# A state-space stage whose convolution moves into TensorE's projection, with the products dt·u·B split between VectorE and GpSimd

## Chip, cores and metric

The kernel runs on one core of a Trainium2 chip. The metric is device time in microseconds (us) of one execution. VectorE (DVE), ScalarE (ACT), GpSimd (POOL) and TensorE (PE) each run their own instructions in order and wait for one another by semaphores.

## What is computed

The program is a decoder of two layers over x of 32 sequences x 128 tokens x 128 channels: attention with 16 heads of 8 channels, a linear-attention block, routed experts, then a state-space layer, attention over a context, and a second set of experts. The change touches the first attention and the state-space layer:

```
# first attention, per head h of 8 channels: rotate q and k, then
scores = q_h @ k_h.T + causal mask ;  softmax ;  @ v_h

# state space, 256 inner channels d, 16 states n, 4 taps
x_in, z = split(layernorm(x) @ W_in)
xc = silu(depthwise_conv(x_in, 4 taps) + conv_b)
dt, B, C = from xc @ W_xproj ;  dt = softplus(dt @ W_dt + b_dt)
h[d,n] = h[d,n] * exp(dt[d] * A[d,n]) + dt[d] * B[n] * xc[d]     # over tokens
y[d] = sum_n h[d,n] * C[n]
out = x + ((y + xc * D) * silu(z)) @ W_out
```

## The kernel before

All six stages keep x in SBUF and take it in 8 groups of 4 sequences (512 tokens). A stage ends with a barrier of all engines.

**State space** (`state_space`, from L1165). The 256 channels are two halves (`ch`) of 128 partitions. One group has 32 steps i, two for each state n: i = 2n + ch. In a step:

- ACT makes the decay exp(dt·A), `m_dA` (L1298). For each n it also copies the row C[n], which PE has spread over the 128 partitions in PSUM, to SBUF, `m_Cs` (L1303).
- DVE makes the input product `m_dBu` (L1371) from B[n] in PSUM and dt·u (`m_DU`) in SBUF, and runs the recurrence as one scan over 512 tokens, `m_h` (L1376). A scan reads two SBUF tensors.
- POOL multiplies `m_h` by `m_Cs` into `m_hC` (L1237), two SBUF tensors again.
- PE adds `m_hC` into PSUM with an identity matmul (L1457) and spreads B and C two states ahead (L1446, L1447).

Depths are: 4 buffers for `m_dA`, `m_h`, `m_Cs`, `m_hC`; 2 PSUM banks for B and 2 for C. `pipeline` (L98) writes one fixed program for each engine: its step i, and after it the stages that `SLOT` puts at i. They prepare group g+1 (projection of z, silus, step sizes), the normalisation and x projection of group g+2, and the end of group g. No engine passes over a stage that waits. The convolution is a part of that: PE projects x_in (L1420), ACT copies it with 3 zero columns ahead of each sequence to `m_xp` (L1263), and DVE does 8 tap operations for a group (L1326 for tap 0, L1329 for the others). ACT then takes silu of z from PSUM (L1268) and of the convolved channels (L1270), with two table loads around them.

**First attention** (`attention` with `cross` false, tiles `a_`). A unit is 8 heads of one sequence, 8 units to a group. PE transposes probabilities (L523), makes scores (L513, two products of 512 columns in two PSUM banks, each over 128 rows with the query masked down to 32 rows by ACT, L300), adds the causal mask (L516) and multiplies by V (L534). DVE takes maxima, differences and sums (L381, L383, L387).

Of the kernel before, what the change touches and what calls it, by code (L numbers as in the profile page):

```python
# [135 lines left out]
def attention(c, tag, cross, W, wsem, wcount, xsem=None, loads=None):  # L136
# [15 lines left out]
    QM = sb("QM", [D, 2, 4, T])  # L152
# [47 lines left out]
    with nc.Block() as block:  # L200
# [263 lines left out]
        def _(pe):  # L464
# [40 lines left out]
            def score(g, par, u):  # L505
# [659 lines left out]
def state_space(c, W, wsem, wcount, out):  # L1165
# [49 lines left out]
    with nc.Block() as block:  # L1215

        @block.gpsimd
        def _(pool):
# [4 lines left out]

# [6 lines left out]

            def step(g, par, i, left):
                n = i // CH
                pool.wait_ge(s["h"], g * NI + i + 1)
# [803 lines left out]
```

## Time and profile before

| what | value |
|---|---|
| median of 3 runs | 2588.0 us (2585.68 to 2591.71) |
| the profiled execution: its time, its span | 2586.46 us, 2584.6 us |
| first attention | 0 to about 360 us of the span |
| linear attention and routed experts | to about 883 us |
| state space | 883 to about 1732 us |
| context attention and second experts | to the end |
| busy: PE, DVE, ACT, POOL | 68%, 74%, 35%, 30% |
| mean granted TensorE clock | 0.832 of 2.4 GHz |

Busy time is summed by engine; an instruction counts as busy also while it is held up inside, after its start. A value of 1.00 in the clock column is 2.4 GHz, 0.50 would be 1.2 GHz.

### The profile page before, as it was taken

What the parts mean: (1) busy time and instruction counts of PE and PEld (TensorE: products, weight loads), DVE (VectorE), ACT (ScalarE), POOL (GpSimd) and SP (SyncE); (2) the same over time, 40 slices, a digit from 0 to 9 for tenths busy, and PEclk for the clock granted to TensorE, in tenths of its full rate; (3) what the DMA queues carried; (4) which work ended last, traced back from release to release, by engine and by line L of the source; (5) the groups of instructions that cost most, each with busy time, mean ns of one, the idle gap of its engine ahead of it and who ended that gap; (6) DMA issues with size and microseconds to landing.
All of it is one profiled execution on the core that took longest, in us unless ns stands there. A gap on an engine that the chain in (4) does not pass through costs nothing. (4 is left out here: it accounts for less than half of the span.)

```text
span 2584.6 us, 29874 instructions
## 1 busy us (share of the span) xinstructions
PE 1767.3 (68%) x9169; PEld 1072.0 (41%) x9169; DVE 1922.4 (74%) x3496; ACT 909.4 (35%) x1342; POOL 776.4 (30%) x739
## 2 busy tenths in 40 slices
PE   6999975655599755656657557558998411488880
PEld 3666655555466411221222212226666411255550
DVE  3888866677578679999999999968999355533335
ACT  2554531221154343434334334325554211122220
POOL 2222112122100034544545544452221000144442
PEclk9999987777699877878778778779999555699995
DMA  3000000000000000000000000000000500011113
GB/s 110 1 0 0 1 11 5 0 5 0 0 1 0 1 0 1 1 0 0 0 0 0 0 0 1 1 5 6 5 5 1 171 0 0 12 33 33 34 32 102
DMA packets 38286, 37.42 MB, mean 14 GB/s; under 512 B 7672, under 2 KB 33281, under 8 KB 37681
## 3 DMA queue, kind: packets, MB, share of 16 engines
q1 hardware_dynamic: 33648, 26.99, 3.4%
q0 software_dynamic: 4544, 9.32, 1.2%
q8 instruction: 44, 0.72, 0.1%
q14 instruction: 50, 0.40, 0.1%
HBM read 25.08 MB, written 11.21 MB: 14 GB/s over the span
## 5 line engine op out<-in xcount | busy, mean ns | idle before, releaser
L1457 PE MATMUL PS<-m_hC,identf 128*128 128x512 f32 x512 | 341.1, 759 | 255.1 <-POOL m_hC L1237 204.3
L1237 POOL TENSOR_TENSOR m_hC<-m_h,m_Cs 128x512 f32<-128x512 f32 x256 | 346.4, 1357 | 365.9 <-DVE m_h L1376 313.8
L1376 DVE TENSOR_TENSOR_SCAN m_h<-m_dA,m_dBu 128x512 f32<-128x512 f32 x256 | 433.0, 1692 | 10.4
L1457 PEld LDWEIGHTS PS<-m_hC,identf 128*128 128x128 f32 x512 | 98.5, 224 | 430.5 <-POOL m_hC L1237 343.0
L1303 ACT COPY m_Cs<-PS 128x512 f32<-128x512 f32 x128 | 74.6, 583 | 352.4 <-PE PS L1447 352.4
L1298 ACT ACTIVATE m_dA<-m_DT,m_A 128x508 f32<-128x508 f32 x256 | 177.6, 717 | 48.5 <-DVE m_h L1376 44.7
L1371 DVE TENSOR_TENSOR m_dBu<-PS,m_DU 128x512 f32<-128x512 f32 x256 | 170.1, 664 | 5.4 <-PE PS L1446 5.2
L1587 POOL DMA_INDIRECT e_XG<-token_rows,e_ids x71 | 68.9, 971 | 239.7 <-DVE e_ids L1723 218.4
L1736 DVE TENSOR_TENSOR e_H<-PS,e_Sg 128x512 f32<-128x512 f32 x71 | 49.1, 692 | 111.2 <-PE PS L1825 90.9
L513 PE MATMUL PS<-a_BD,a_QM 128*128 128x512 f32 x256 | 123.1, 604 | 3.1 <-ACT a_QM L300 3.1
L82 POOL TENSOR_TENSOR ln_lv<-ln_mv,ln_eps 128x4 f32<-128x4 f32 x40 | 8.0, 200 | 363.2 <-DVE ln_mv L75 363.2
L1631 ACT ACTIVATE e_Sg<-PS 128x512 f32<-128x512 f32 x71 | 42.4, 597 | 196.2 <-PE PS L1824 192.7
L1592 POOL DMA_INDIRECT expert_rows<-e_Yo,e_ids x71 | 70.0, 985 | 133.4 <-DVE e_Yo L1742 131.0
L311 ACT COPY a_PT<-PS 128x1024 f32<-128x1024 f32 x63 | 63.8, 1012 | 104.9 <-PE PS L523 104.9
L1446 PE MATMUL PS<-m_hi,w_sel 96*128 96x512 bf16 x128 | 59.8, 467 | 46.8 <-DVE m_dBu L1371 43.8
L381 DVE TENSOR_REDUCE a_mx<-PS 128x8 f32<-128x1024 f32 x64 | 77.3, 1208 | 11.9 <-PE PS L516 11.9
L311 ACT COPY k_PT<-PS 77x1024 f32<-77x1024 f32 x63 | 63.4, 1007 | 60.3 <-PE PS L523 60.3
L387 DVE TENSOR_REDUCE a_sm<-a_E 128x8 f32<-128x1024 f32 x64 | 77.4, 1210 | 9.5 <-ACT a_E L272 9.5
L272 ACT ACTIVATE a_E<-a_DD 128x1024 f32<-128x1024 f32 x64 | 67.7, 1057 | 41.1 <-DVE a_DD L383 39.7
L1824 PE MATMUL PS<-e_w_wg,e_xT 128*128 x142 | 80.3, 648 | 0.0
L523 PE MATMUL PS<-identf,k_E 128*77 128x128 f32 x512 | 69.8, 279 | 15.4 <-ACT k_E L272 15.3
L383 DVE TENSOR_TENSOR a_DD<-PS,a_mx 128x1024 f32<-128x1024 f32 x64 | 78.4, 1224 | 2.2
(342 smaller groups left out, 4135.7 us busy)
## 6 DMA issues: line engine op xcount, KB each, us to landing
token_rows<-X SPq DMA_DIRECT2D x2, 2048.0 KB, 12.6
e_Y<-expert_rows SPq DMA_DIRECT2D x16, 256.0 KB, 3.6
e_w_wg<-in_w_wg SPq DMA_DIRECT2D x1, 2048.0 KB, 8.1
e_w_wu<-in_w_wu SPq DMA_DIRECT2D x1, 2048.0 KB, 12.5
e_w_wd<-in_w_wd SPq DMA_DIRECT2D x1, 2048.0 KB, 16.9
out_dram<-X SPq DMA_DIRECT2D x8, 256.0 KB, 2.3
X<-in_x SPq DMA_DIRECT2D x1, 1792.0 KB, 7.2
x_Cs<-in_ctx SPq DMA_DIRECT2D x8, 154.0 KB
```

What stands on the lines that cost most here:

```text
L311: nc.scalar.copy(PT[:, u % 2], PS[0:KL, 4:6, :].rearrange("p i (h q) -> p (i h) q", q=P)).then_inc(s["pt"], 1)
L381: nc.vector.tensor_reduce(m, units(hf), AX_X, ALU.max).then_inc(s["mx"], 1)
L383: nc.vector.tensor_tensor(d, units(hf), mb, ALU.subtract).then_inc(s["d"], 1)
L387: nc.vector.tensor_reduce(sm[:, u * HU:(u + 1) * HU], E[:, u % 2], AX_X, ALU.add).then_inc(s["sm"], 1)
L513: ins = nc.tensor.matmul(scores(gp), QM[:, par, gp, b * P:(b + 1) * P], BD[:, par, :, b, :], start=True, stop=cross)
L1237: nc.gpsimd.tensor_tensor(hC[:, i % ND, :], hst[:, i % ND, :], Cs[:, n % ND, :], ALU.mult).then_inc(s["hC"], 1)
L1298: nc.scalar.activation(dA[:, i % ND, :, 1:P], bl(DT[:, par, ch, :])[:, :, 1:P], ACT.Exp, scale=A[:, ch, n:n + 1]).then_inc(s["dA"], 1)
L1303: nc.scalar.copy(Cs[:, n % ND, :], bank(3 + n % 2)).then_inc(s["Cs"], 1)
L1371: nc.vector.tensor_tensor(dBu[:, i % 2, :], bank(1 + n % 2), DU[:, par, ch, :], ALU.mult).then_inc(s["dBu"], 1)
L1376: nc.vector.tensor_tensor_scan(hst[:, i % ND, :], dA[:, i % ND].rearrange("p b l -> p (b l)"), dBu[:, i % 2, :], 0.0, ALU.mult, ALU.add).t ...
L1457: nc.tensor.matmul(bank(5 + ch), c.identf[:, :], hC[:, i % ND, :], start=(n == 0), stop=(n == NS - 1)).then_inc(s["yacc"], 1)
L1824: nc.tensor.matmul(bank(GATE[i % 2]), xT[:, i % 2, :], one(W["wg"][:, bass.ds(e, 1), :]), start=True, stop=True).then_inc(s["gu"], 1)
```

## The change

1. The convolution goes into PE. With `m_Wc[k]` = W_in times tap k, the x projection is four accumulating matmuls per half over `m_xnT` shifted by k (the three zero columns now stand in `m_xnT`). The 8 tap operations, `m_U` and the copies to `m_xp` are gone. The taps' weights are a new load of 512 KB (`w4_cwr`), issued when the stage begins, and POOL multiplies them by W_in once.
2. The projections change place: z first (slot 8), copied by ACT to SBUF (slot 9), then x (slot 10) in the same two banks, and both silus at slot 13, x's from PSUM.
3. ACT copies B[n] to SBUF, `m_Bs` (4 buffers), behind the copy of C[n].
4. DVE makes `m_dBu` from `m_Bs` for half 0 only; POOL makes that of half 1, for state n+1 between its two `m_hC` of state n.
5. The two normalisations of the stage use scalar_tensor_tensor with the reciprocal root broadcast, in place of tensor_scalar.
6. In the first attention the query is no longer masked: POOL writes it once, and each score product takes 32 of the 128 rows, at rows 32·gp. ACT's four copies for a group are gone.

```diff
-    QM = sb("QM", [D, 2, 4, T])
+    QM = sb("QM", [D, 2, 4, T] if cross else [D, 2, T])
...
                 for gp in (2 * hf, 2 * hf + 1):
-                    ins = nc.tensor.matmul(scores(gp), QM[:, par, gp, b * P:(b + 1) * P], BD[:, par, :, b, :], start=True, stop=cross)
+                    r = slice(0, D) if cross else slice(32 * gp, 32 * gp + 32)
+                    q = QM[r, par, gp, b * P:(b + 1) * P] if cross else QM[r, par, b * P:(b + 1) * P]
+                    ins = nc.tensor.matmul(scores(gp), q, BD[r, par, :, b, :], start=True, stop=cross)
...
-    SLOT = {"gated": 3, "output": 0, "residual": 5, "rstd": 4, "norm": 7, "project_z": 8, "silus": 13, "dt_b_c": 11,
+    SLOT = {"gated": 3, "output": 0, "residual": 5, "rstd": 4, "norm": 7, "project_z": 8, "z_copy": 9, "project_x": 10, "silus": 13, "dt_b_c": 14,
...
+            def other_input(g, par, n):
+                pool.wait_ge(s["du"], g + 1)
+                pool.wait_ge(s["Bs"], g * NS + n + 1)
+                if not first(g, n, 2):
+                    pool.wait_ge(s["h"], g * NI + CH * (n - 1))
+                nc.gpsimd.tensor_tensor(dBu[:, 1, n % 2, :], Bs[:, n % ND, :], DU[:, par, 1, :], ALU.mult).then_inc(s["dBu1"], 1)
...
+            def z_copied(g, par):
+                for ch in range(CH):
+                    act.wait_ge(s["z"], g * CH + ch + 1)
+                    nc.scalar.copy(SZ[:, par, ch, :], bank(AUX[ch])).then_inc(s["zc"], 1)
...
             def silus(g, par):
                 for ch in range(CH):
-                    act.wait_ge(s["z"], g * CH + ch + 1)
-                    nc.scalar.activation(SZ[:, par, ch, :], bank(AUX[ch]), ACT.Silu).then_inc(s["sz"], 1)
-                act.wait_ge(s["cv"], g * 8 + 8)
-                nc.scalar.activation(U2[:, par], U[:, :, :], ACT.Silu).then_inc(s["u"], 1)
+                    act.wait_ge(s["xpc"], g * CH + ch + 1)
+                    nc.scalar.activation(U2[:, par, ch, :], bank(AUX[ch]), ACT.Silu, bias=W["cb"][:, ch:ch + 1]).then_inc(s["u"], 1)
+                act.wait_ge(s["zc"], g * CH + CH)
+                nc.scalar.activation(SZ[:, par], SZ[:, par], ACT.Silu).then_inc(s["sz"], 1)
...
+                    nc.scalar.copy(Bs[:, n % ND, :], bank(1 + n % 2)).then_inc(s["Bs"], 1)
...
-                nc.vector.tensor_tensor(dBu[:, i % 2, :], bank(1 + n % 2), DU[:, par, ch, :], ALU.mult).then_inc(s["dBu"], 1)
+                if ch == 0:
+                    dve.wait_ge(s["Bs"], g * NS + n + 1)
+                    nc.vector.tensor_tensor(dBu[:, 0, n % 2, :], Bs[:, n % ND, :], DU[:, par, 0, :], ALU.mult).then_inc(s["dBu0"], 1)
+                else:
+                    dve.wait_ge(s["dBu1"], g * NS + n + 1)
...
+            def project_x(g, par):
+                for ch in range(CH):
+                    pe.wait_ge(s["zc"], g * CH + ch + 1)
+                    for k in range(DC):
+                        ins = nc.tensor.matmul(bank(AUX[ch]), Wc[:, k, ch * P:(ch + 1) * P], xnT[:, :, k:k + P], start=(k == 0), stop=(k == DC - 1))
+                    ins.then_inc(s["xpc"], 1)
```

POOL's order in the first steps of group 0: before, the eight products `m_hC` follow one another.

```order
L84 TENSOR_TENSOR m_irs<-m_ilv,ln_half 128x4
L1237 TENSOR_TENSOR m_hC<-m_h,m_Cs 128x512 x8
```

Now (`m_dBu` is the input product of half 1, one state ahead):

```order
L1241 TENSOR_TENSOR m_dBu<-m_Bs,m_DU 128x512
L1251 TENSOR_TENSOR m_hC<-m_h,m_Cs 128x512
L1241 TENSOR_TENSOR m_dBu<-m_Bs,m_DU 128x512
L1251 TENSOR_TENSOR m_hC<-m_h,m_Cs 128x512 x2
L1241 TENSOR_TENSOR m_dBu<-m_Bs,m_DU 128x512
L1251 TENSOR_TENSOR m_hC<-m_h,m_Cs 128x512 x2
```

POOL has three products for each state instead of two.

ACT's order at slots 9 to 13 of a group, inside the loop. Before, only decays and copies of C stand between slots 9 and 13, and the silus follow the decay (`m_dA`) of i = 13:

```order
L1298 ACTIVATE m_dA<-m_DT,m_A 128x4x127
L1267 ISA
L1268 ACT_TABLE_LOAD
L1268 ACTIVATE m_SZ<-PS 128x512
L1267 REGISTER_ALU
L1268 ACTIVATE m_SZ<-PS 128x512
L1269 ISA
L1270 ACTIVATE m_U<-m_U 128x1024
L1271 ACT_TABLE_LOAD
```

Now the copies of z stand behind the decay of i = 9, ahead of the decay of i = 10 and of C[5] and B[5]:

```order
L1317 ACTIVATE m_dA<-m_DT,m_A 128x4x127
L1281 ISA
L1282 COPY m_SZ<-PS 128x512
L1281 REGISTER_ALU
L1282 COPY m_SZ<-PS 128x512
L1316 REGISTER_ALU
L1317 ACTIVATE m_dA<-m_DT,m_A 128x4x127
L1319 REGISTER_ALU
L1321 REGISTER_ALU
L1322 COPY m_Cs<-PS 128x512
L1325 REGISTER_ALU
L1327 COPY m_Bs<-PS 128x512
```

ACT has got two places (the second is slot 13) at which it waits for PE's projections before it can copy the next B.

PE's order at slot 10, now (L1463 and L1464 spread B and C, L1474 adds `m_hC`, L1437 is the x projection); before, two matmuls L1420 stood in a group's x projection, at slot 24:

```order
L1463 MATMUL PS<-m_hi,w_sel 128x512
L1464 MATMUL PS<-m_hi,w_sel 128x512
L1435 ISA
L1437 MATMUL PS<-m_xnT,m_Wc 128x512 x4
L1435 REGISTER_ALU
L1437 MATMUL PS<-m_xnT,m_Wc 128x512 x4
L1473 REGISTER_ALU
L1474 MATMUL PS<-m_hC,identf 128x512
```

Eight matmuls stand there in one piece, behind the `m_hC` of i = 10 and ahead of that of i = 11.

## Rows read from the trace of the kernel before

**Rows 1.** State space: PE, PEld, DVE, ACT, POOL busy us; granted clock, DMA share.

```profile
883.00:1732.00 849.00, 516.12 (x1088) 182.16 (x1088) 793.94 (x872) 331.71 (x507) 391.09 (x300) 0.78 0.00 0
```

**Rows 2.** Groups of the page: busy us, mean ns, idle before and its releaser.

```profile
L1237 POOL TENSOR_TENSOR m_hC<-m_h,m_Cs 128x512 f32<-128x512 f32 x256 | 346.4, 1357 | 365.9 <-DVE m_h L1376 313.8
...
L1371 DVE TENSOR_TENSOR m_dBu<-PS,m_DU 128x512 f32<-128x512 f32 x256 | 170.1, 664 | 5.4 <-PE PS L1446 5.2
```

**Rows 3.** The scans by their tile: ns min/median/max, first and last start.

```profile
L1376 DVE TENSOR_TENSOR_SCAN m_h<-m_dA,m_dBu x256: 1224/1808/2872, 932.3 to 1715.3; 128x512 f32<-128x512 f32 x128
```

**Rows 4.** Timeline of POOL and DVE, a regular step: start us, duration us.

```profile
1229.53 0.66 DVE L1371 TENSOR_TENSOR m_dBu<-PS,m_DU 128x512 f32<-128x512 f32 x1
1229.83 1.27 POOL L1237 TENSOR_TENSOR m_hC<-m_h,m_Cs 128x512 f32<-128x512 f32 x1 [3.95 <-DVE m_h L1376]
1230.23 1.95 DVE L1376 TENSOR_TENSOR_SCAN m_h<-m_dA,m_dBu 128x512 f32<-128x512 f32 x1
...
1232.26 1.26 POOL L1237 TENSOR_TENSOR m_hC<-m_h,m_Cs 128x512 f32<-128x512 f32 x1 [1.16 <-DVE m_h L1376]
```

**Rows 5.** Timeline of POOL and DVE where both have work at once.

```profile
1253.37 1.56 POOL L1237 TENSOR_TENSOR m_hC<-m_h,m_Cs 128x512 f32<-128x512 f32 x1
...
1254.49 1.52 DVE L1376 TENSOR_TENSOR_SCAN m_h<-m_dA,m_dBu 128x512 f32<-128x512 f32 x1
...
1254.90 2.17 POOL L1237 TENSOR_TENSOR m_hC<-m_h,m_Cs 128x512 f32<-128x512 f32 x1
```

**Rows 6.** Timeline of DVE, the eight taps of a group.

```profile
1217.91 3.02 DVE L1326 TENSOR_SCALAR m_U<-m_xp,w_cw,w_cb 128x512 f32<-128x512 f32 x2
1220.85 1.40 DVE L1329 SCALAR_TENSOR_TENSOR m_U<-m_xp,w_cw,m_U 128x512 f32<-128x512 f32 x2
...
1224.03 3.72 DVE L1329 SCALAR_TENSOR_TENSOR m_U<-m_xp,w_cw,m_U 128x512 f32<-128x512 f32 x4
```

**Rows 7.** Timeline of ACT at slot 13.

```profile
956.09 0.58 ACT L1303 COPY m_Cs<-PS 128x512 f32<-128x512 f32 x1 [1.78 <-PE PS L1447]
956.57 0.72 ACT L1298 ACTIVATE m_dA<-m_DT,m_A 128x508 f32<-128x508 f32 x1
...
958.60 1.08 ACT L1268 ACTIVATE m_SZ<-PS 128x512 f32<-128x512 f32 x2
959.57 1.06 ACT L1270 ACTIVATE m_U<-m_U 128x1024 f32<-128x1024 f32 x1
960.65 1.28 ACT L1271 ACT_TABLE_LOAD   x1
```

**Rows 8.** Timeline of PE, projections (a matmul of this type has two records).

```profile
889.57 3.78 PE L1420 MATMUL PS<-m_xnT,w_win 128*128 128x512 f32 x4 [0.93 <-ACT m_xnT L1258]
...
955.89 1.88 PE L1420 MATMUL PS<-m_xnT,w_win 128*128 128x512 f32 x4
```

**Rows 9.** Timeline of POOL, a product of 1024 columns.

```profile
916.19 2.34 POOL L1229 TENSOR_TENSOR m_DU<-m_DT,m_U 128x1024 f32<-128x1024 f32 x1 [29.94 <-DVE m_DT L1362]
```

**Rows 10.** The page's DMA issues: KB each, median us to landing.

```profile
e_Y<-expert_rows SPq DMA_DIRECT2D x16, 256.0 KB, 3.6
```

**Rows 11.** First attention: busy time by engine in one group's stretch.

```profile
157.23:196.75 39.52, 39.52 (x273) 24.58 (x272) 34.62 (x44) 20.43 (x23) 9.40 (x10) 1.00 0.00 0
```

**Rows 12.** First attention: timelines of PE and of DVE's waits.

```profile
153.16 1.07 PE L534 MATMUL PS<-a_PT,a_V 128*32 128x128 f32 x16
154.16 1.09 PE L523 MATMUL PS<-identf,a_E 128*128 128x128 f32 x8
155.08 1.88 PE L513 MATMUL PS<-a_BD,a_QM 128*128 128x512 f32 x4
156.80 0.60 PE L516 MATMUL PS<-w_cmask,identb 128*128 128x512 bf16 x2
...
158.94 0.69 DVE L443 TENSOR_TENSOR a_oT<-PS,a_rT 128x512 f32<-128x512 f32 x1 [1.68 <-PE PS L534]
...
192.63 1.22 DVE L387 TENSOR_REDUCE a_sm<-a_E 128x8 f32<-128x1024 f32 x1 [1.30 <-ACT a_E L272]
```

More of the change, by code:

```diff
@@ L92, in ln_apply, with ln_apply_fused @@
     ins.then_inc(done, 1)
+def ln_apply_fused(dve, nc, out, src, ln, s, n, done):
+    dve.wait_ge(s["rs"], n)
+    for b in range(GB):
+        ins = nc.vector.scalar_tensor_tensor(out[:, b, :], src[:, b, :], ln["mv"][:, b, 0:1], ln["rs"][:, b:b + 1].to_broadcast([P, D]),
+                                             ALU.subtract, ALU.mult)
+    ins.then_inc(done, 1)
 LN_SEMS = "st mv lv rs"
@@ L1303, in step @@
                     nc.scalar.copy(Cs[:, n % ND, :], bank(3 + n % 2)).then_inc(s["Cs"], 1)
-            pipeline(act, SLOT, SH, NI, setup, {"xn_copy": normalised, "xp_copy": convolved}, {"silus": silus, "parts": parts, "dt_bias": step_sizes, "logs": logs}, step, {})
+                    act.wait_ge(s["B"], g * NS + n + 1)
+                    if not first(g, n, ND):
+                        act.wait_ge(s["dBu0"], g * NS + n - ND + 1)
+                        act.wait_ge(s["dBu1"], g * NS + n - ND + 1)
+                    nc.scalar.copy(Bs[:, n % ND, :], bank(1 + n % 2)).then_inc(s["Bs"], 1)
+            pipeline(act, SLOT, SH, NI, setup, {"xn_copy": normalised}, {"z_copy": z_copied, "silus": silus, "parts": parts, "dt_bias": step_sizes, "logs": logs}, step, {})
         @block.vector
@@ L1410, in transposed, with project_z @@
                 ins.then_inc(s["xnp"], 1)
-            def project(first_chunk, done, read):
-                def stage(g, par):
-                    for ch in range(CH):
-                        if read:
-                            pe.wait_ge(s[read], g * CH + ch + 1)
-                        elif ch == 0:
-                            pe.wait_ge(s["xnT"], g + 1)
-                        i = first_chunk + ch
-                        nc.tensor.matmul(bank(AUX[ch]), W["win"][:, i * P:(i + 1) * P], xnT[:, :], start=True, stop=True).then_inc(s[done], 1)
-                return stage
+            def project_z(g, par):
+                pe.wait_ge(s["xnT"], g + 1)
+                for ch in range(CH):
+                    nc.tensor.matmul(bank(AUX[ch]), W["win"][:, (CH + ch) * P:(CH + ch + 1) * P], xnT[:, :, DC - 1:DC - 1 + P], start=True, stop=True).then_inc(s["z"], 1)
+            def project_x(g, par):
+                for ch in range(CH):
+                    pe.wait_ge(s["zc"], g * CH + ch + 1)
+                    for k in range(DC):
+                        ins = nc.tensor.matmul(bank(AUX[ch]), Wc[:, k, ch * P:(ch + 1) * P], xnT[:, :, k:k + P], start=(k == 0), stop=(k == DC - 1))
+                    ins.then_inc(s["xpc"], 1)
             def dt_b_c(g, par):
-                pe.wait_ge(s["u"], g + 1)
+                pe.wait_ge(s["u"], g * CH + CH)
                 for ch in range(CH):
```

96 lines of the change are left out of this document (42 added, 54 removed).

## The prediction

> **What bounds it now.** I read the busy times by stretch first. In the state-space stage DVE is busy 793.94 of 849 us, 94%, POOL 391 and ACT 332 [rows 1]. That looks like a stage that VectorE's work bounds, and the change takes 128 input products and 56 to 64 tap operations from VectorE. So I looked at what DVE's busy time consists of. The scans last 1.22 us at least and 1.81 at the median [rows 3]: a third of such a scan is not work. The regular step shows why [rows 4]. The product `m_dBu` starts at 1229.53 and lasts 0.66, although `m_hC` runs on POOL from 1229.83 to 1231.10. The scan starts at 1230.23 and ends at 1232.18, 1.08 behind the end of `m_hC`; the next `m_hC` starts 0.08 after that. So the scan does not run while `m_hC` does, and the product, which reads one tensor from PSUM and one from SBUF, does. Scan and `m_hC` alternate on something shared; the 0.66 of the product costs nothing, since it lies under `m_hC`. A step takes 0.70 (product to scan) plus a scan of 1.81 to 1.95 less 0.08 of overlap: 2.43 to 2.57, mean 2.5, and 32 steps 80 us.
>
> POOL waits as well when it comes second [rows 5]. An `m_hC` started at 1253.37, behind a scan in flight, takes 1.56. The scan of 1254.49 ends at 1256.01, 1.08 behind it. The `m_hC` of 1254.90 takes 2.17 and ends at 1257.07, 1.06 behind the scan. When both have work they go in turn, a scan for 1.08 and a POOL product for 1.06. PE, busy 516 of the 849 us [rows 1], is not what ends these waits: 314 of POOL's 366 us of idle time end on the scan [rows 2].
>
> The Trainium skill (SBUF — State Buffer, Who interferes with whom) says the same as a rule: a VectorE instruction with two SBUF inputs and a GpSimd instruction that reads SBUF exclude each other for their whole length, and one with a single SBUF input is free of this. By that rule, and by the sentences above without it, a copy of B in SBUF takes VectorE's product out of its cover. The sum by rows and by rule is one.
>
> **The change, part by part.**
>
> *Regular states.* For each n, DVE has a product and two scans, POOL three products, and now all six read two SBUF tensors. DVE's product is not shown with two SBUF inputs. Its price is between 0.66 [rows 4], alone, and 0.66 less the 0.14 that a scan loses from 1.22 to 1.08 when its start is already behind it, 0.52. I take 0.55, since it will wait for POOL's product as the scan does. One state: 2 x 1.08 + 0.55 + 3 x 1.06 = 5.89 us against 2 x 2.5 = 5.00 now. That is 0.89 x 16 = 14.3 us a group, 114 for eight. If the order let DVE and POOL each take two turns at once it would be 3 x 1.27 + 2.7, 6.4; if they went free of each other, 3.8: bounds +180 and -150.
>
> *Taps.* A group's eight start at 1217.91 and take, without what overlaps, 2.9 + 1.3 + 3.7 = 8 us [rows 6]. About 2 us of the first pair is a wait for the product `m_DU` on POOL, which the next DVE instruction will now have, and 1 us a wait for an `m_hC`, of which half would be there anyway. I take 5.5 us. Two of the eight sets stand ahead of the first scan; six in the loop give -33.
>
> *ACT's two waits.* This is the part whose cost isn't in any busy time. Until now ACT was up to 4 decays ahead. z's copies stand behind decay 9, and PE comes to z only behind the `m_hC` of step 8. Chain from the end of scan 8: `m_hC` behind scan 9, 1.08 + 1.06; PE's identity matmul 0.9 and the two spreads 0.5; z's two matmuls at 0.86 each (the four records to 957.6 take 1.72 [rows 8]), ACT's last copy 0.58, decay 0.72, C 0.58, B 0.58 [rows 7]; with some 0.4 for six handovers, 8.1 us. DVE has in it scan 9, POOL the `m_hC` of 8. The shared path lies idle from the end of that `m_hC`, 2.2 us in, until B[5] comes: 5.8 us. At slot 13 ACT waits for both x projections. From the end of `m_hC` 10: 0.9 + 0.5, eight matmuls 6.9, the second silu of x 0.6, z's 1.06, the table load 1.28, then 0.72 + 0.58 + 0.58 for B[7], with handovers 13.4 us. State 6 covers 5.9 of it, 7.5 are idle. Sum 13.3 us in each of the seven groups that prepare a next one, +93. Before, the same silus and loads were there and hidden by ACT's lead. Behind ACT's wait stand decays 10 and 14 too, but the scans want B first. Lower bound 0, if the lead of two PSUM banks of B and 4 of `m_Bs` holds; it can't, as every copy is behind the wait in ACT's order.
>
> *PE's clock.* The stage has 0.78 on average [rows 1], so nearly half of it is at 1.2 GHz. There a projection costs twice: the four records of 889.57 take 3.78 against 1.88 [rows 8]. The eight matmuls may start at the lower level. I add 1 us a group for that, +7; bounds 0 and 7 x 6.9 = 48.
>
> *ACT's 128 copies of B*, 0.58 each, 75 us: ACT has 849 - 332 idle, hidden outside the two waits. *Normalisations:* 128 columns in another instruction, 64 of them, taken at 0 (bounds -4 and +13 from 0.2 each).
>
> *The stage's start.* POOL's first reciprocal root now waits for the taps' load, more than the 3.6 us of 256 KB [rows 10], I take 4.5, and a product of 1024 columns, 2.34 [rows 9]. Six matmuls more at the low level cost 10 us in each of two groups, partly behind each other; the taps (6 us in a set), the copies ahead of them and the unshared silu go. Net +3, bounds -5 and +12.
>
> *First attention.* PE is busy 39.52 of 39.52 us, DVE 34.62 [rows 11], so PE bounds it. Two score products take 1.72 of 4.2 us of a unit [rows 12]. Their row blocks now differ and so do their banks. Whether two products of 32 rows run side by side the trace doesn't show. Nearest: L534's eight products of 128 columns, in column blocks, take 1.00 (153.16 to 154.16), and at 0.86 for 512 columns they would take 1.72 one by one. So blocks do overlap two by two. Then a pair takes 0.86, PE 39.5 - 8 x 0.86 = 32.6, and DVE bounds: 34.6 + 0.4 of gaps + the waits that aren't PE's (1.30 for the last exponential; the 1.68 of L443 shrinks) = 36.6. So -2.9 for seven groups, -20, and -7 ahead of the first group, where four masking operations and slow scores go: -27. Without overlap -3. The skill (TensorEngine Tiling (Array Packing), Tiling Modes) lists 32 x 128 as four independent tiles; as far as column blocks go the rows agree, and by its rule the figure would be the same -27, as DVE bounds then.
>
> **Sum:** 114 - 33 + 93 + 7 + 3 - 27 = +157 us. Against the profiled execution's 2586.5 that is 2743.5, and the median of the runs is 1.5 above it: **2745 us**.
>
> **Rivals.**
> - *VectorE's work bounds* (faster). DVE loses 128 x 0.66 = 84 us and some 44 of taps, attention 27: 2433 us. For it: DVE's 94%. Against: 1.81 against 1.22 [rows 3], that is 150 us of waiting inside DVE's busy time. It would take that `m_dBu` from SBUF and POOL's products don't exclude each other or the scans, which rows 4 and 5 speak against. It decides if a state takes under 5.0 us. 0.06.
> - *ACT keeps its lead* and only the alternation costs: 2745 - 93 - 7 = 2645. For it: 4 buffers of B. 0.14.
> - *Scores don't overlap:* 2745 + 24 = 2769. 0.17.
> - *PE at the low clock in its long piece*: +41, 2786, or both of the last. 0.08.
> - The forecast: 0.55.
>
> **How the numbers follow.** The range 2640 to 2800 holds all but the first rival and the tails. Changes of under 0.2% can't be told from none here. Faster 0.06, same 0.01, slower 0.93. The likeliest case alone reaches from 2715 to 2775.
>
> **What will show it.** Regular states of 5.9 us, with scans at a median of 2.2 and `m_hC` mostly over 2; POOL and DVE both idle some 6 and 7.5 us once each in a group, ended by ACT's `m_Bs`, while ACT waits for z's and x's projection; a group of 120 to 126 us; the stage about 1030 long; attention groups of 36.6. Wrong would be: scans of 1.22, DVE's product at 0.69 under a running POOL product, or no idle stretch at slots 9 and 13.

## The result, and the profile after

The changed kernel takes 2783.17 us (median of 4 runs, 2780.37 to 2785.59) against 2586.84 us of the kernel before in the same comparison (4 runs, 2585.37 to 2591.71): ratio 1.0755, 95% interval 1.0742 to 1.0768. It is 7.6% slower. The forecast was 2745 us; the measured time lies 38 us above it, inside the range of 2640 to 2800 and outside the 2715 to 2775 of the likeliest case alone. The profiled execution has a span of 2778.6 us and a mean granted clock of 0.787.

I read the stretches first, as in [rows 1] and [rows 11]. State space, and one group of the first attention, after (PE, PEld, DVE, ACT, POOL busy us; granted clock, DMA share):

```profile
861.00:1925.00 1064.00, 665.98 (x1184) 228.03 (x1184) 826.65 (x680) 393.11 (x635) 765.22 (x429) 0.68 0.00 1
157.00:194.20 37.20, 35.21 (x273) 20.92 (x272) 34.34 (x44) 17.97 (x19) 9.36 (x11) 1.00 0.00 0
```

The state-space stage has 192 VectorE instructions fewer (680 against 872) and lasts 215 us longer. VectorE's busy time went up by 33 us for them, GpSimd's nearly doubled, from 391 to 765. The attention group is 2.3 us shorter. The groups of the page that answer to [rows 2], and the instructions on the tile `m_h` (ns min/median/max, first and last start), of which the scans answer to [rows 3]:

```profile
L1251 POOL TENSOR_TENSOR m_hC<-m_h,m_Cs 128x512 f32<-128x512 f32 x256 | 506.8, 1993 | 69.4 <-DVE m_h L1391 69.4
...
L1384 DVE TENSOR_TENSOR m_dBu<-m_Bs,m_DU 128x512 f32<-128x512 f32 x128 | 165.6, 1294 | 168.3 <-ACT m_Bs L1327 168.0
L1241 POOL TENSOR_TENSOR m_dBu<-m_Bs,m_DU 128x512 f32<-128x512 f32 x128 | 205.6, 1606 | 174.5 <-ACT m_Bs L1327 152.1
```

```profile
L1391 DVE TENSOR_TENSOR_SCAN m_h<-m_dA,m_dBu x256: 1191/2018/2290, 907.0 to 1905.3; 128x512 f32<-128x512 f32 x128
L1251 POOL TENSOR_TENSOR m_hC<-m_h,m_Cs x256: 1255/2175/2191, 909.3 to 1908.5; 128x512 f32<-128x512 f32 x128
```

Half as many input products on VectorE cost as much busy time (165.6 us) as all 256 did before (170.1). One takes 1294 ns in place of 664. And two idle times that were not there before, 168 us on VectorE and 152 on GpSimd, end with ScalarE's copy of B. These are the two prices of the forecast: the turns that VectorE and GpSimd take when both read two tensors from SBUF, and ScalarE's waits.

A regular state, timeline of DVE and POOL (as [rows 4]):

```profile
1418.63 1.68 DVE L1384 TENSOR_TENSOR m_dBu<-m_Bs,m_DU 128x512 f32<-128x512 f32 x1
1419.73 1.71 POOL L1241 TENSOR_TENSOR m_dBu<-m_Bs,m_DU 128x512 f32<-128x512 f32 x1
...
1420.50 4.15 DVE L1391 TENSOR_TENSOR_SCAN m_h<-m_dA,m_dBu 128x512 f32<-128x512 f32 x2 [0.19 <-DVE m_dBu L1384]
1421.40 4.32 POOL L1251 TENSOR_TENSOR m_hC<-m_h,m_Cs 128x512 f32<-128x512 f32 x2
...
1424.58 1.69 DVE L1384 TENSOR_TENSOR m_dBu<-m_Bs,m_DU 128x512 f32<-128x512 f32 x1
```

Neither engine is idle for more than 0.2 us, and each of the six instructions is held by the one of the other engine. From product to product it is 5.95 us. Slot 9 of a group, the chain of the forecast, timeline of all engines (TensorE's weight loads left out):

```profile
1323.40 2.09 POOL L1251 TENSOR_TENSOR m_hC<-m_h,m_Cs 128x512 f32<-128x512 f32 x1 [2.51 <-DVE m_h L1391]
1325.54 1.12 PE L1474 MATMUL PS<-m_hC,identf 128*128 128x512 f32 x2 [3.48 <-POOL m_hC L1251]
...
1326.94 3.58 PE L1431 MATMUL PS<-m_xnT,w_win 128*128 128x512 f32 x4
1328.84 0.59 ACT L1282 COPY m_SZ<-PS 128x512 f32<-128x512 f32 x1 [13.54 <-PE PS L1431]
...
1331.03 0.72 ACT L1317 ACTIVATE m_dA<-m_DT,m_A 128x508 f32<-128x508 f32 x1
...
1332.12 0.60 ACT L1327 COPY m_Bs<-PS 128x512 f32<-128x512 f32 x1
...
1332.75 0.69 DVE L1384 TENSOR_TENSOR m_dBu<-m_Bs,m_DU 128x512 f32<-128x512 f32 x1 [8.32 <-ACT m_Bs L1327]
1332.79 1.77 POOL L1241 TENSOR_TENSOR m_dBu<-m_Bs,m_DU 128x512 f32<-128x512 f32 x1 [7.30 <-ACT m_Bs L1327]
```

GpSimd and VectorE wait 7.3 us together for one copy of 0.6 us that stands behind ScalarE's wait of 13.5 us. Forecast were 5.8. At slot 13 the same happens, now for the x projection and the silus:

```profile
1341.14 7.03 PE L1437 MATMUL PS<-m_xnT,m_Wc 128*128 128x512 f32 x16
...
1348.21 0.69 ACT L1287 ACTIVATE m_U<-PS,w_cb 128x512 f32<-128x512 f32 x1 [2.75 <-PE PS L1437]
1348.79 1.04 ACT L1289 ACTIVATE m_SZ<-m_SZ 128x1024 f32<-128x1024 f32 x1
...
1349.86 1.28 ACT L1290 ACT_TABLE_LOAD   x1
...
1352.90 1.78 POOL L1241 TENSOR_TENSOR m_dBu<-m_Bs,m_DU 128x512 f32<-128x512 f32 x1 [7.90 <-ACT m_Bs L1327]
```

7.9 us idle, forecast 7.5. This is the fourth group. In the seven groups that prepare another, the stretches at slot 9 are 5.7, 7.3, 8.4, 7.3, 8.1, 8.3 and 8.0 us and those at slot 13 are 7.6, 8.9, 7.6, 7.9, 9.2, 7.7 and 7.8 (from the timelines of VectorE and GpSimd), 110 us together where the forecast had 93. The two projections by their lines (ns min/median/max), the first line of x, the second of z:

```profile
L1437 PE MATMUL PS<-m_xnT,m_Wc x112: 590/591/1057, 948.9 to 1740.4; 128*128 128x512 f32 x112
```

```profile
L1431 PE MATMUL PS<-m_xnT,w_win x28: 590/1036/1061, 936.6 to 1723.0; 128*128 128x512 f32 x28
```

The long piece of x ran at 2.4 GHz nearly throughout; of z's matmuls most took the longer of the two times, 3.58 us for the pair of projections against 1.88 in [rows 8]. The granted clock, the value before the last two of each row, is 0.54 in the stretch of z's pair and 1.00 in that of x's eight matmuls (columns as at the top):

```profile
1326.90:1330.60 3.70, 3.61 (x5) 0.97 (x4) 0.00 (x0) 0.64 (x2) 0.00 (x0) 0.54 0.00 0
...
1341.10:1348.20 7.10, 7.10 (x18) 3.21 (x18) 2.84 (x2) 0.69 (x1) 2.74 (x2) 1.00 0.00 0
```

### The profile page after: what moved, and what is told of

It is laid out like the page before. It is cut to its first block and busy times, and to the rows that moved or that the text cites. A ratio compares the mean times of both kernels' runs of the same rounds, so it can differ in the third digit from the quotient of the medians.

```text
span 2778.6 us, 30271 instructions
## 1 busy us (share of the span) xinstructions
PE 1889.5 (68%) x9265; PEld 1090.4 (39%) x9265; DVE 1953.6 (70%) x3304; ACT 951.4 (34%) x1438; POOL 1150.2 (41%) x868
## 5 line engine op out<-in xcount | busy, mean ns | idle before, releaser
L1474 PE MATMUL PS<-m_hC,identf 128*128 128x512 f32 x512 | 422.0, 931 | 365.4 <-POOL m_hC L1251 323.6
L1251 POOL TENSOR_TENSOR m_hC<-m_h,m_Cs 128x512 f32<-128x512 f32 x256 | 506.8, 1993 | 69.4 <-DVE m_h L1391 69.4
L1391 DVE TENSOR_TENSOR_SCAN m_h<-m_dA,m_dBu 128x512 f32<-128x512 f32 x256 | 467.4, 1863 | 19.4 <-DVE m_dBu L1384 18.3
L1474 PEld LDWEIGHTS PS<-m_hC,identf 128*128 128x128 f32 x512 | 114.4, 267 | 584.7 <-POOL m_hC L1251 513.5
L1384 DVE TENSOR_TENSOR m_dBu<-m_Bs,m_DU 128x512 f32<-128x512 f32 x128 | 165.6, 1294 | 168.3 <-ACT m_Bs L1327 168.0
L1241 POOL TENSOR_TENSOR m_dBu<-m_Bs,m_DU 128x512 f32<-128x512 f32 x128 | 205.6, 1606 | 174.5 <-ACT m_Bs L1327 152.1
L82 POOL TENSOR_TENSOR ln_lv<-ln_mv,ln_eps 128x4 f32<-128x4 f32 x40 | 11.1, 278 | 344.1 <-DVE ln_mv L75 344.1
L522 PE MATMUL PS<-identf,k_E 128*77 128x128 f32 x512 | 69.8, 279 | 15.5 <-ACT k_E L278 15.4
L512 PE MATMUL PS<-k_BD,k_QM 128*128 128x308 f32 x256 | 78.4, 429 | 0.0
```

The source lines that it names most:

```text
L512: ins = nc.tensor.matmul(scores(gp), q, BD[r, par, :, b, :], start=True, stop=cross)
L1241: nc.gpsimd.tensor_tensor(dBu[:, 1, n % 2, :], Bs[:, n % ND, :], DU[:, par, 1, :], ALU.mult).then_inc(s["dBu1"], 1)
L1384: nc.vector.tensor_tensor(dBu[:, 0, n % 2, :], Bs[:, n % ND, :], DU[:, par, 0, :], ALU.mult).then_inc(s["dBu0"], 1)
L1391: nc.vector.tensor_tensor_scan(hst[:, i % ND, :], dA[:, i % ND].rearrange("p b l -> p (b l)"), dBu[:, ch, n % 2, :], 0.0, ALU.mult, ALU.ad ...
L1474: nc.tensor.matmul(bank(5 + ch), c.identf[:, :], hC[:, i % ND, :], start=(n == 0), stop=(n == NS - 1)).then_inc(s["yacc"], 1)
```

## The experiments

One table serves several of them: the length of each state of the fourth group, from the start of an even scan to that of the next, in us (worked out from the timelines; state n is steps 2n and 2n+1; states 2, 5, 10 to 12 and 15 are left out). It shows one group. The other middle groups are alike in most rows but not in all: state 8 of e2 is 5.5 here and 4.3 at the median of the seven groups, state 9 is 4.9 here and 6.0 there.

| state | before | after | e8 split alone | e2 slots | e4 fold | e5 fold, slots | e9 |
|---|---|---|---|---|---|---|---|
| 0 | 4.9 | 6.0 | 6.0 | 6.0 | 4.9 | 4.9 | 7.0 |
| 1 (gated product, but e9) | 8.5 | 9.9 | 9.9 | 9.9 | 8.5 | 8.5 | 4.5 |
| 3 (normalisation) | 6.9 | 8.2 | 8.0 | 8.2 | 7.0 | 7.0 | 6.3 |
| 4 (slot 9) | 4.4 | **11.5** | 4.1 | 4.1 | **9.4** | 4.4 | 4.4 |
| 6 (slot 13) | 4.4 | **12.9** | 4.9 | 4.9 | **9.0** | 4.4 | 4.4 |
| 7 (inner normalisation) | 6.9 | 9.9 | 9.7 | 9.9 | 6.5 | 7.0 | 7.2 |
| 8 | 4.4 | 4.1 | 4.1 | 5.5 | 4.4 | 5.9 | 5.1 |
| 9 | 5.0 | 6.0 | 6.0 | 4.9 | 5.0 | 5.0 | 4.4 |
| 13 | 5.0 | 6.0 | 6.0 | 6.0 | 5.0 | 4.4 | 4.4 |
| 14 (step sizes, taps) | 17.4 | 13.3 | 19.0 | 13.3 | 11.1 | 11.1 | 8.7 |
| whole group | 102.5 | 129.6 | 119.4 | 113.5 | 105.8 | 99.0 | 91.1 |

The kernel before took 2587.2 us in the comparison of e1 to e4, 2587.1 for e5 to e8, 2589.7 for e9 to e11 and 2587.2 for e12. A difference between runs of two comparisons, as of e9 or e10 from e5, carries some 3 us of this.

**e1, the attention's part alone.** The kernel before with `attention` as changed (the edit is the first two pieces of the diff above; GpSimd writes the query once, and ScalarE's masking copies are gone).

> The kernel before with only the first attention's part of the change (query not masked, each score product over 32 rows). Theory 1 (score products of two row blocks overlap, VectorE then bounds a group): in the changed kernel a group of this stage lasts 37.2 us against 39.5 and the stage ends some 20 us earlier, so 2567 us, and the state-space stage keeps its 849 us and its clock of 0.78. Rival (the 20 us come back as a colder or later state space, or are no saving at all): 2587. Rival (full overlap, as forecast): 2560.

Measured: 2566.8 us, ratio 0.9918 (0.9896 to 0.9939). The 20.4 us are those of theory 1. The state-space stage behind it is unchanged: from the first scan to the end of the last it takes 784.8 us in both kernels, at a mean clock of 0.78. That two score products of 32 rows run side by side is to be seen in the timeline of PE after:

```profile
165.08 1.13 PE L512 MATMUL PS<-a_BD,a_QM 32*128 32x512 f32 x4
166.14 0.61 PE L515 MATMUL PS<-w_cmask,identb 128*128 128x512 bf16 x2
```

The pair takes 1.06 us to the next matmul, against 1.72 in [rows 12]. The forecast had 0.86.

**e8, the split alone.** The kernel before with the copy of B and half 1 on GpSimd; taps, slots and normalisations as they were.

```diff
+                    nc.scalar.copy(Bs[:, n % ND, :], bank(1 + n % 2)).then_inc(s["Bs"], 1)
...
+                nc.gpsimd.tensor_tensor(dBu[:, 1, n % 2, :], Bs[:, n % ND, :], DU[:, par, 1, :], ALU.mult).then_inc(s["dBu1"], 1)
...
-                nc.vector.tensor_tensor(dBu[:, i % 2, :], bank(1 + n % 2), DU[:, par, ch, :], ALU.mult).then_inc(s["dBu"], 1)
+                    nc.vector.tensor_tensor(dBu[:, 0, n % 2, :], Bs[:, n % ND, :], DU[:, par, 0, :], ALU.mult).then_inc(s["dBu0"], 1)
```

> The kernel before with the split of the input products alone (copy of B, half 1 on GpSimd); convolution, slots, normalisations and attention as before. Theory 1: regular states 5.96 against 5.0, 123 us, no idle stretches of ScalarE's making, the taps a little longer since they share with three GpSimd products: 2587 + 123 + 0 to 25 = 2710 to 2735. Rival (the loss is the fold's, the split relieves VectorE): 2640 or less. Rival (the order of turns differs with the taps there): above 2750.

Measured: 2717.8 us, ratio 1.0504 (1.0484 to 1.0525), +130.7. Regular states take 5.95 us where before has 5.0, and there is no idle stretch at slots 9 and 13. So moving half of the products off VectorE costs 131 us by itself.

There is a third place at which ScalarE's copy of B is late, and the forecast had no term for it. Before state 13, ScalarE waits for TensorE's step sizes (3.69 and 1.02 us) and normalised transposes (2.19 us) ahead of the copy. VectorE and GpSimd stand idle there in six groups, 2.4 to 3.1 us each and 17 us together, and state 12 takes 7.2 us where before has 4.4. The input product behind the stretch, timeline of GpSimd:

```profile
1372.34 1.77 POOL L1237 TENSOR_TENSOR m_dBu<-m_Bs,m_DU 128x512 f32<-128x512 f32 x1 [3.08 <-ACT m_Bs L1323]
```

The stretch of the stage also bears on the clock (columns as above):

```profile
883.00:1862.00 979.00, 614.42 (x1088) 203.65 (x1088) 875.04 (x740) 390.35 (x635) 755.24 (x426) 0.69 0.00 0
```

TensorE issues the 1088 matmuls of [rows 1], and its mean clock falls from 0.78 to 0.69. The lower clock after, 0.68, thus does not need the folded convolution: here the same matmuls are spread over a longer stage, and e4 and e5, which have the folded convolution's 1184 matmuls and no split, have 0.76 and 0.78.

**e3, VectorE's product reads B from PSUM.** One word of the changed kernel, and a guard on the bank:

```diff
-                    nc.vector.tensor_tensor(dBu[:, 0, n % 2, :], Bs[:, n % ND, :], DU[:, par, 0, :], ALU.mult).then_inc(s["dBu0"], 1)
+                    nc.vector.tensor_tensor(dBu[:, 0, n % 2, :], bank(1 + n % 2), DU[:, par, 0, :], ALU.mult).then_inc(s["dBu0"], 1)
...
+                    pe.wait_ge(s["dBu0"], g * NS + n - 1)
```

> The changed kernel, VectorE's product of half 0 reads B from its PSUM bank (behind ScalarE's copy, as now, so that it starts at the same point) instead of from the copy in SBUF; one wait of TensorE is added to guard the bank. Theory 1 (two SBUF inputs exclude the product while GpSimd works, PSUM and SBUF do not): a regular state loses the product's turn, 5.96 to 5.3 or 5.4 us, 128 states give 70 to 85 us, 2700 to 2715, with the product at 0.66 under a running GpSimd product. Rival (the product is on VectorE's own path and costs its 0.66 whatever it reads): 2783, states of 5.96.

Measured: 2728.6 us, ratio 1.0545 (1.0526 to 1.0564): 54.6 us less than the changed kernel. Direction as theory 1, size below it. A regular state, timeline of DVE and POOL:

```profile
1338.96 2.10 POOL L1251 TENSOR_TENSOR m_hC<-m_h,m_Cs 128x512 f32<-128x512 f32 x1 [2.25 <-DVE m_h L1391]
1339.92 0.67 DVE L1384 TENSOR_TENSOR m_dBu<-PS,m_DU 128x512 f32<-128x512 f32 x1
1340.77 1.38 DVE L1391 TENSOR_TENSOR_SCAN m_h<-m_dA,m_dBu 128x512 f32<-128x512 f32 x1 [0.19 <-DVE m_dBu L1384]
1341.03 2.18 POOL L1241 TENSOR_TENSOR m_dBu<-m_Bs,m_DU 128x512 f32<-128x512 f32 x1
...
1343.40 2.12 DVE L1391 TENSOR_TENSOR_SCAN m_h<-m_dA,m_dBu 128x512 f32<-128x512 f32 x1 [1.25 <-POOL m_dBu L1241]
```

The product is 0.67 again, under a running `m_hC`. But it lets the scan start earlier, GpSimd's product for the other half is then held behind that scan, and the second scan waits 1.25 us for it. The state is 5.51 us, not 5.3 to 5.4. ScalarE's two waits are still there, and the states with slots 9 and 13 are longer than in the changed kernel (12.8 and 14.1 us in the fourth group).

**e6, both products from the copy, GpSimd untouched.** The kernel before with ScalarE's copy of B, read by VectorE for both halves.

```diff
+                    nc.scalar.copy(Bs[:, n % ND, :], bank(1 + n % 2)).then_inc(s["Bs"], 1)
...
-                nc.vector.tensor_tensor(dBu[:, i % 2, :], bank(1 + n % 2), DU[:, par, ch, :], ALU.mult).then_inc(s["dBu"], 1)
+                nc.vector.tensor_tensor(dBu[:, i % 2, :], Bs[:, n % ND, :], DU[:, par, ch, :], ALU.mult).then_inc(s["dBu"], 1)
```

> The kernel before with only ScalarE's copy of B to SBUF; VectorE still makes both halves' input products, now from that copy, and GpSimd does what it did. Theory 1 (two SBUF inputs on VectorE and a GpSimd product exclude each other): the input product no longer lies under the running m_hC, a step goes from 2.5 us to 1.27 + 0.55 to 0.66 + 1.22 = 3.05 to 3.15, 256 steps give +140 to +165, 2725 to 2755. Rival (only the scan is held, a product is not): 2587 to 2600.

Measured: 2669.7 us, ratio 1.0318 (1.0298 to 1.0338), +82.7. Neither theory's number. The timeline shows who gives way:

```profile
1235.91 0.67 DVE L1376 TENSOR_TENSOR m_dBu<-m_Bs,m_DU 128x512 f32<-128x512 f32 x1
1236.21 1.48 POOL L1238 TENSOR_TENSOR m_hC<-m_h,m_Cs 128x512 f32<-128x512 f32 x1 [2.02 <-DVE m_h L1381]
1236.61 2.17 DVE L1381 TENSOR_TENSOR_SCAN m_h<-m_dA,m_dBu 128x512 f32<-128x512 f32 x1
1238.70 0.66 DVE L1376 TENSOR_TENSOR m_dBu<-m_Bs,m_DU 128x512 f32<-128x512 f32 x1
```

They do exclude each other, but the product is not held: it stands right behind the scan in VectorE's order and goes first, at its 0.67. `m_hC`, which starts 0.30 later, is held instead (1.48 for 1.27 before), and the scan behind it (2.17 for 1.95). From product to product a step is 2.79 us, 0.29 more, not 0.55. The rule of the Trainium skill (SBUF — State Buffer, Who interferes with whom) that whoever issues first gets the shared access agrees with this order.

**e2, ScalarE's waits three steps later.** The changed kernel with

```diff
-    SLOT = {..., "z_copy": 9, "project_x": 10, "silus": 13, "dt_b_c": 14,
+    SLOT = {..., "z_copy": 12, "project_x": 10, "silus": 16, "dt_b_c": 15,
```

> The changed kernel, ScalarE's copy of z moved from slot 9 to 12, its silus from 13 to 16, and TensorE's dt, B, C projection from 14 to 15. Nothing is added or taken away, only ScalarE's waits for TensorE's projections stand three steps later in its order. Theory 1 (those waits hold up the copies of B, 7.3 and 7.9 us in a group): both idle stretches shrink to under 2 us each, seven groups get back 11 to 15 us each, 2680 to 2705. Rival (TensorE's extra work or its clock costs the time, whichever engine waits for it): 2783 within 10. Regular states stay at 5.96 in both.

Measured: 2662.0 us, ratio to before 1.0288 (1.0269 to 1.0306): 121 us less than the changed kernel, for three numbers in a table. That is more than theory 1's 78 to 103 us. States 4 and 6 fall from 11.5 and 12.9 to 4.1 and 4.9, that is 15.4 us in this group; over the seven groups it is 112 us, and state 12 gives 8 more, as the stretch before state 13 shrinks too (16.3 us in all after, 8.5 in e2). Waits of ScalarE and VectorE in the stage (us in total, times, longest), after:

```profile
ACT m_SZ L1282 <- PE PS L1431: 103.2, 16, 14.9
ACT m_U L1287 <- PE PS L1437: 81.0, 16, 9.4
...
DVE m_dBu L1384 <- ACT m_Bs L1327: 168.0, 29, 10.3
```

and in e2:

```profile
ACT m_SZ L1282 <- PE PS L1431: 12.7, 15, 2.2
...
DVE m_dBu L1384 <- ACT m_Bs L1327: 38.0, 19, 4.4
```

TensorE's work is the same in both. What it cost was decided by where another engine stood waiting for it. The clock went up with the shorter stage, from 0.68 to 0.72.

**e4, the fold without the split**, and **e5, the same with e2's slots.** The input products are those of before, from PSUM on VectorE (e8's diff reversed, in the changed kernel).

> The changed kernel with the input products as before (both halves on VectorE from PSUM, no copy of B), so the folded convolution, its slots and the attention remain. Theory 1: states are back at 5.0 us, -123; ScalarE's two waits now hold up decays and copies of C but no B, so the idle stretches shrink by two copies (1.2 us) each or more; the taps stay away. 2783 - 123 - 17 to - 60: 2600 to 2643. Rival (the eight-matmul projection and the lower clock are the cost, the split costs nothing): 2740 or more. Rival (the split is all of the cost): under 2560, since taps and attention then give 33 and 20 against 2587.

> The kernel with the folded convolution and the old input products, and the three slots of the experiment before moved too (z's copy 12, silus 16, dt/B/C 15). Theory 1: in the fold alone a group of the middle has two states of 9.4 and 9.0 us where before has 4.4 and 4.4, both at ScalarE's waits; they fall to 5 or less, seven times some 9 us, 2591 - 60 = 2531 (2520 to 2545). Rival (the lower clock or the eight matmuls in one piece delay everything anyway): 2570 or more.

Measured: e4 2591.4 us, ratio 1.0015 (1.0006 to 1.0025); e5 2540.9 us, ratio 0.9821 (0.9802 to 0.9840). e4 is 9 us below its range: without the copy of B, ScalarE's waits are cheaper than I had allowed, 50 us instead of 121, as they hold up only decays and copies of C. They still cancel what the taps and the attention give. e5 is 1.8% faster than before. From e1's 2566.8 to e5 the fold gives 26 us. A part of ScalarE's wait is left in e5: state 8, where the silus now stand, takes 5.9 us against 4.4 in e4, and its second scan starts after 2.2 us of idle time, just behind a decay that follows the silus and their table load.

**e7, the normalisations as before.** The changed kernel with `ln_apply` in place of `ln_apply_fused`.

> The changed kernel with the two normalisations as before (tensor_scalar). In the changed kernel's trace their 64 instructions take 64 us against 41.8 before, and the state with the inner one lasts 9.9 us against 6.9. Theory 1 (the broadcast reciprocal root is a second SBUF tensor, so that each of the four waits for a turn of GpSimd): 22 us of busy time and about 2 us of each group come back, 2761 to 2773. Rival (they are long only since GpSimd now has three products, and would be so in the old form): 2780 to 2785.

Measured: 2782.3 us, ratio to before 1.0755 (1.0730 to 1.0781), no change from 2783.2. Theory 1 falls. The groups of the inner one, after and in e7:

```profile
L98 DVE SCALAR_TENSOR_TENSOR m_Xn<-X,m_imv,m_irs 128x128 f32<-128x128 f32 x32 | 33.3, 1098 | 13.3 <-POOL m_irs L84 13.3
```

```profile
L90 DVE TENSOR_SCALAR m_Xn<-X,m_imv,m_irs 128x128 f32 x24 | 29.7, 1295 | 5.0 <-POOL m_irs L84 5.0
```

The first line is of all 32 instructions, and 8 of them, ahead of the loop, take 0.35 us each; the second is of the 24 inside the loop alone. Inside the loop they take 1.35 us in the new form, 1.30 in the old one, and 0.80 in the kernel before. The split without the new form (e8) has the same length:

```profile
L90 DVE TENSOR_SCALAR m_Xn<-X,m_imv,m_irs 128x128 f32 x24 | 29.7, 1296 | 5.0 <-POOL m_irs L84 5.0
```

So it comes with the split, and belongs to its price.

**e9, fewer instructions with two SBUF inputs.** On e5: VectorE also makes `m_hC` of half 1, with C from its PSUM bank, and both input products of state n+1 between its two scans.

```diff
+                if i % CH:
+                    return
                 pool.wait_ge(s["h"], g * NI + i + 1)
...
+                if ch == 0:
+                    if n + 1 < NS:
+                        products(g, par, n + 1)
...
+                    nc.vector.tensor_tensor(hC[:, i % ND, :], hst[:, i % ND, :], bank(3 + n % 2), ALU.mult).then_inc(s["hC1"], 1)
...
-    SLOT = {"gated": 3,
+    SLOT = {"gated": 1,
```

> From the kernel with the folded convolution and moved slots (2541). What shares SBUF is cut down instead of moved: VectorE makes m_hC of half 1 itself, with C read from its PSUM bank, and both input products of the next state, B from PSUM, stand between its two scans; GpSimd keeps m_hC of half 0. TensorE spreads B behind the even step and C behind the odd one, and the gated product stands at slot 1. Theory 1 (only instructions with two SBUF inputs exclude each other): under GpSimd's one product of 1.27 lie two of VectorE's of 0.66, a state is 2 x 1.22 + 3 x 0.66 = 4.4 to 4.5 us against 5.0, so -0.5 x 128 = -64, 2477 (2460 to 2505). Rival (VectorE's work bounds at once, and its 0.66 comes on top of 5.0): states of 5.6, 2610. Rival (C's new chain over VectorE, TensorE and ScalarE is late): 2541 or more, with VectorE idle for m_Cs.

Measured: 2494.6 us, ratio 0.9631 (0.9607 to 0.9654). A state from its timeline:

```profile
1189.71 1.22 DVE L1375 TENSOR_TENSOR_SCAN m_h<-m_dA,m_dBu 128x512 f32<-128x512 f32 x1
1190.84 1.26 DVE L1365 TENSOR_TENSOR m_dBu<-PS,m_DU 128x512 f32<-128x512 f32 x2
1191.16 1.28 POOL L1243 TENSOR_TENSOR m_hC<-m_h,m_Cs 128x512 f32<-128x512 f32 x1 [5.75 <-DVE m_h L1375]
1192.02 1.50 DVE L1375 TENSOR_TENSOR_SCAN m_h<-m_dA,m_dBu 128x512 f32<-128x512 f32 x1
1193.55 0.69 DVE L1386 TENSOR_TENSOR m_hC<-m_h,PS 128x512 f32<-128x512 f32 x1
```

From even scan to even scan it is 4.45 us, with three of the four products on the engine that looked full. The one on GpSimd runs beside two from PSUM. This run changes several things at once (C from PSUM, the order of the products, where TensorE spreads B and C, the gated product's place). The gain over e5 is 46 us; e11 shows that the gated product's place alone gives 15. How the rest is shared out was not tried; e3 has the change to one PSUM operand by itself.

**e10, the x projection twice**, and **e11, the gated product at slot 1**, both on e5.

```diff
-                    for k in range(DC):
+                    for k in (*range(DC), *range(DC)):
```

> The kernel with the folded convolution and moved slots (2541), with the four matmuls of each half of the x projection issued twice (the second set overwrites the bank with the same sums), so TensorE has 8 more matmuls of 0.59 to 0.86 us in one piece of each group. Theory 1 (TensorE's work costs only where an engine waits for it in its order; ScalarE's silus now stand six steps behind): 0 to +15, 2541 to 2556. Rival (TensorE's extra work is on the path): 7 x 4.7 to 6.9 = 33 to 48 more, 2574 to 2589.

> The kernel with the folded convolution and moved slots (2541), with VectorE's gated product at slot 1 in place of 3. In its trace the state with the gated product lasts 8.5 us, of which 5.0 are the state and 2.6 the two instructions, so some 0.9 us is a wait for TensorE, which spreads B[2] only behind the gated product. Theory 1: that wait goes, seven groups give 5 to 12 us, 2529 to 2536. Rival (the wait moves to the sums of the last state, which the gated product needs): 2541 or more.

Measured: e10 2590.7 us, ratio 1.0009 (0.9997 to 1.0020), 50 us above e5: the rival's side, and my theory 1 as I stated it falls. A piece of 13.8 us is longer than TensorE's lead of two states. Timeline of the place in e10:

```profile
1270.77 1.88 PE L1451 MATMUL PS<-m_hC,identf 128*128 128x512 f32 x4
...
1272.91 0.69 DVE L1363 TENSOR_TENSOR m_dBu<-PS,m_DU 128x512 f32<-128x512 f32 x1 [4.26 <-PE PS L1440]
```

One piece of 6.9 us was hidden (state 7 lasts 7.0 in e5, 6.9 before, and the excess of e5's state 8 is the silus'); one of 13.8 us leaves VectorE 4.3 us without B. The seven groups are 39 us longer together, and the first scan starts 9 us later (915.3 us into the execution against 905.9). e11 took 2526.3 us, ratio 0.9757 (0.9741 to 0.9774), 14.6 us below e5; I had expected 5 to 12.

**e12, the x projection in two pieces**, on e9: half 0 at slot 10, half 1 at slot 12.

> The fastest kernel so far (2495, m_hC of half 1 on VectorE) with the x projection in two pieces of four matmuls, half 0 at slot 10 and half 1 at slot 12. Its state with slot 15 lasts 7.2 to 9.7 us in the groups that prepare another, where 4.4 are the state, 2.2 to 2.5 the normalisation, and the rest waits for TensorE behind its eight matmuls. Theory (after the doubled projection cost 50 us: one piece of 7 us uses up the lead, the amount of work does not matter): the state falls to 7 or less and the one behind it from 5.1 to 4.4, seven groups give 8 to 18 us, 2477 to 2487. Rival (the amount counts, wherever it stands): 2490 to 2500.

Measured: 2495.0 us, ratio 0.9645 (0.9632 to 0.9659), the time of e9: the rival's number, but for another reason. State 7 falls from 7.2 to 5.5 us, and state 8 grows from 5.1 to 8.3:

```profile
1229.42 1.28 ACT L1277 ACT_TABLE_LOAD   x1
...
1230.71 1.33 ACT L1304 ACTIVATE m_dA<-m_DT,m_A 128x508 f32<-128x508 f32 x2
1231.52 1.22 DVE L1375 TENSOR_TENSOR_SCAN m_h<-m_dA,m_dBu 128x512 f32<-128x512 f32 x1 [3.85 <-issue]
```

The 3.85 us of idle time have no releaser in the view. The decay of the same step ends just ahead of the scan: with TensorE out of the way, the scan waits for the decay that stands behind the silus and the table load in ScalarE's order. The wait was moved and not removed.

## Why the prediction was right, and where it was short

The direction and both mechanisms hold. Set against the terms of the sum, the runs give:

| term | forecast | measured | from |
|---|---|---|---|
| split: regular states | +114 | +131 | e8 - before |
| ScalarE's two waits, and TensorE's clock in them | +93 +7 | +121 | after - e2 |
| taps, stage's start, normalisations | -33 +3 | -35 | e2 - e8, less e1's 20: what is left |
| first attention | -27 | -20 | e1 - before |
| sum | +157 | +196 | from the unrounded times |

The right column adds up by construction, as the runs form a chain from before to after; that it closes shows nothing. The third row has support of its own: state 14, which held the taps, falls from 19.0 us in e8 to 13.3 in e2, 34 us in the six groups inside the loop (forecast 33). The first scan starts 27 us earlier in e2 than in e8, 24 of it e1's, so the stage's start gave some 3 us where I had +3. What the other states gain and lose cancels to 2 us.

*Regular states.* 5.89 us forecast, 5.95 measured. Scans have a median of 2.02 (forecast 2.2), `m_hC` one of 2.18 (mean 1.99). The price of one such state was right, but multiplying it by 16 was not, and that the total comes near (114 against 131) is in part luck. Over seven groups of e8 against before, the seven states 0 to 3, 5, 9 and 13 are longer by 1.0 us each on average, states 6 and 10 by 0.5, and states 4, 8 and 15 are not longer at all. The four states 7, 11, 12 and 14 are longer by 2.3 on average. State 7 holds the inner normalisation (9.7 us in e8, 6.9 before), whose cost I had put at nothing, bounds -4 and +13, for the wrong reason: e7 shows that the form of the instruction is free, and e8's rows that both forms are longer beside a third GpSimd product. State 12 holds the third wait for B, 17 us that no term had. (In the forecast's upper bound 3 x 1.27 + 2.7 is 6.5 and not 6.4, which makes it +193 instead of +180; nothing hung on it.)

*ScalarE's two waits.* This is the term that was mis-sized most, 100 against 121 us. The two stretches sum to 110 us over seven groups where I had 93; in the group shown they are 7.3 and 7.9 us where I had 5.8 and 7.5. The 1.5 at slot 9 is TensorE's clock: I took z's pair at the 1.72 of a row at 2.4 GHz and added 1 us a group to the eight matmuls of x for a low clock. It was the other way round: x ran at 591 ns a record, z's pair took 3.58 us at a granted clock of 0.54. Before that TensorE had stood idle for 3.48 us, waiting for `m_hC`. By states, after less e2 is 54 us in state 4, 58 in state 6 and 8 in state 12, the third wait for B; the rest of the group gives 3 back.

*Rivals.* "ACT keeps its lead" (2645) is e2's case, which had to be made by hand and took 2662. "VectorE's work bounds" would have made e8 faster; it is 131 us slower. "PE at the low clock in its long piece" had 2786, near the measured time, but its mechanism is not what happened: 112 records of the long piece have a median of 591 ns. "Scores don't overlap" is excluded by 1.06 against 1.72, though a quarter of the overlap's gain was missing (why, no run shows): 8 x 0.66 us of PE a group and not 8 x 0.86, so that VectorE's and TensorE's work are both close to the group's 37.2 us (34.3 and 35.2).

*What would show it.* A group lasts 129.6 to 132.4 us in the middle (forecast 120 to 126), the stage 1064 (1030), attention groups 37.2 (36.6); the idle stretches are ended by `m_Bs` while ScalarE waits for z and x, as said.

*Open.* At slot 3 TensorE's spread of B stands behind the gated product. Whether that costs the changed kernel what e11 gives e5 wasn't tried.

## What to carry to other kernels

Before moving work from a busy engine to an idle one, see what its busy time consists of: here a third of a scan was waiting for the idle engine's own instructions, and the product to be moved was the one instruction that ran beside them. In products and scans of this kind (fp32, 128 x 512), count VectorE's instructions with two SBUF inputs and GpSimd's as one queue, and shorten that queue: an operand left in PSUM took an instruction out of it (e3, and with other edits e9), a copy to SBUF put it in (e6, e8). And a stage that makes an engine wait is paid for by what is queued behind the wait; three numbers in a slot table were worth 121 us (e2), more than the convolution's whole gain.

## What I had not expected of the hardware

- Who is held depends on who was already waiting. In e6 GpSimd's product is released only by the scan's end and starts 0.30 us behind VectorE's: VectorE's costs its bare 0.67 us, and GpSimd's is held. After the change GpSimd's `m_hC` is already waiting when the scan ends, and VectorE's product takes 1.69 us (1424.58 in the regular state above). In e6 the exclusion costs 0.29 us a step, not the length of the added instruction.
- Two fp32 products of 32 rows x 512 columns, in different row blocks and PSUM banks, took 1.06 us together; two of 128 rows take 1.72. The overlap isn't complete.
- The mean granted clock fell from 0.78 to 0.69 with the same 1088 matmuls (e8), issued over 979 us in place of 849.
